# Layers two and three of the last MLP as fp32r products in a two-layer graph network kernel

## The reference

```python
def conv(x, a, eps, W, b):               # GIN block
    ax = a @ x
    h = ax + (1.0 + eps[0]) * ax
    for i in range(3):
        h = relu(h @ W[i].T + b[i])
    return h
merged = concatenate((conv(x, adj, eps1, W1, b1), conv(x2, adj, eps2, W2, b2)), axis=1)
x = layernorm(x + merged @ Wm.T + bm)    # layer 0 of the network
A = adj + eye(4096); deg = A.sum(axis=1)
d = where(deg > 0, rsqrt(deg), 0)
x = layernorm(x + ((d[:, None] * A * d[None, :]) @ x) @ W.T + b)   # layer 1
```

## Time and profile before

| | |
|---|---|
| median of three runs | 594.1 us |
| the profiled execution's own time | 593.58 us |
| its span in the trace | 591.8 us |
| TensorE busy | 584.8 us (99%) |
| VectorE busy | 540.5 us (91%) |
| ScalarE busy | 372.2 us (63%) |
| mean granted TensorE clock | 0.997 |

### The profile page before, as it was taken

How to read it: one execution, slowest core, us unless ns; L and a number is a source line. 1 busy time by engine, 2 the same in 40 slices (tenths; PEclk the granted TensorE clock), 3 DMA queues, 4 the chain that set the end, 5 groups by cost and what they waited for, 6 DMA issues and landing times.

```text
span 591.8 us, 7721 instructions
## 1 busy us (share of the span) xinstructions
PE 584.8 (99%) x2676; PEld 484.3 (82%) x2676; DVE 540.5 (91%) x679; ACT 372.2 (63%) x494; POOL 28.7 (5%) x31
## 2 busy tenths in 40 slices
PE   8999999999999999999999999999999999999996
PEld 7888888888888888888888888867888888888885
DVE  6999999997988998998799999994899999989986
ACT  6554446842544773454667336486897888898893
POOL 1000000001100000110000020000200010010011
PEclk9999999999999999999999999999999999999998
DMA  9978565443554533354443375776699999999911
GB/s 334 370 271 296 202 226 197 142 148 137 214 205 170 190 145 142 142 213 174 181 150 138 138 293 189 286 299 212 245 353 413 364 370 383 400 365 374 387 42 71
DMA packets 27849, 141.56 MB, mean 239 GB/s; under 512 B 2608, under 2 KB 3376, under 8 KB 13616
## 3 DMA queue, kind: packets, MB, share of 16 engines
q1 hardware_dynamic: 27248, 139.54, 63.6%
q10 hardware_dynamic: 576, 1.70, 0.7%
HBM read 139.14 MB, written 2.10 MB: 239 GB/s over the span
## 4 chain that ended last, share of the span: by engine, by line
PE 98%; issue 0%; DVE 0%; POOL 0%; POOLq 0%; DVEq 0%
PE ps L468 81%; PE ps L544 7%; PE pd L486 6%; PE pd L497 2%; PE pd L530 1%; PE pd L592 1%; POOLq L118 0%; POOL rstd L1119 0%; DVE z L1090 0%; PE pd L494 0%; DVE stats L1095 0%; DVE outn L1104 0%; POOL identity L1123 0%; DVE mv L897 0%; DVEq L118 0%
## 5 line engine op out<-in xcount | busy, mean ns | idle before, releaser
L649 ACT ACTIVATE ahi<-raw 128x1024 fp32r<-128x1024 f32 x212 | 221.7, 1057 | 165.4 <-PE ps L468 152.8
L816 DVE TENSOR_TENSOR alo<-raw,ahi 128x1024 fp32r<-128x1024 f32 x212 | 257.2, 1220 | 29.7 <-ACT ahi L649 27.9
L468 PE MATMUL ps<-ahi,x2s 128*128 128x512 f32 x512 | 138.4, 389 | 0.0
L468 PE MATMUL ps<-ahi,x1hi 128*128 128x512 f32 x384 | 121.8, 393 | 0.0
L468 PE MATMUL ps<-alo,x1hi 128*128 128x512 f32 x384 | 120.5, 390 | 0.0
L468 PE MATMUL ps<-ahi,x1lo 128*128 128x512 f32 x384 | 120.4, 389 | 0.0
L468 PEld LDWEIGHTS ps<-ahi,x2s 128*128 128x128 f32 x512 | 96.1, 188 | 20.0
L468 PEld LDWEIGHTS ps<-ahi,x1hi 128*128 128x128 f32 x384 | 71.9, 188 | 15.9 <-issue 1.4
L468 PEld LDWEIGHTS ps<-alo,x1hi 128*128 128x128 f32 x384 | 72.0, 188 | 15.2 <-DVE alo L816 0.3
L468 PEld LDWEIGHTS ps<-ahi,x1lo 128*128 128x128 f32 x384 | 72.1, 188 | 14.9
L468 PE MATMUL ps<-alo,x2s 128*128 128x512 f32 x256 | 80.3, 389 | 0.0
(11 more groups left out here) (98 smaller groups left out, 510.7 us busy)
## 6 DMA issues: line engine op xcount, KB each, us to landing
raw<-a_t SPq DMA_DIRECT2D x108, 1024.0 KB, 4.9
raw<-a_t SPq DMA_DIRECT2D x32, 512.0 KB, 7.4
raw<-early SPq DMA_DIRECT2D x7, 512.0 KB, 7.8
xn<-x SPq DMA_DIRECT2D x3, 1024.0 KB, 8.1
out<-outn ACTq DMA_DIRECT2D x3, 512.0 KB, 6.7
par<-params SPq DMA_DIRECT2D x1, 708.0 KB, 12.8
raw<-head SPq DMA_DIRECT2D x2, 256.0 KB, 3.2
xn<-x SPq DMA_DIRECT2D x1, 512.0 KB, 7.2
```

What stands on the lines that cost most here:

```text
L468: mm = pe.matmul(ps[bank + (CH * (q % 2) if layer else 0)][:, :], block_of(w, n), a[c], start=(n == 0 and k == 0), stop=(n == JB - 1 and k ...
L649: act.activation(ring_hi(layer, q, n), raw_tile(layer, n), ACT.Copy).then_inc(hi_ready, 1)
L816: dve.tensor_tensor(ring_lo(layer, q, n), raw_tile(layer, n), as_f32(ring_hi(layer, q, n)), ALU.subtract).then_inc(lo_ready, 1)
```

## The change

In plan 1, dense layer 0 stays a float32 product. Dense layers 1 and 2 become three fp32r passes each. After relu 0 and relu 1 of each part, ScalarE makes a second relu from PSUM with output in fp32r (hhi). VectorE subtracts it from h into h_rest, which lies on h's own place. Slots four and five of the ring of high parts get memory of their own instead of hhi's, one of them on the place of rowsum_all; rounding of tile 5 therefore waits for the transpose, which moves from VectorE's step 4 to step 1, and the reduction from 5 to 2.

TensorE's dense layers come after tiles 1, 3 and 5 and the merge after tile 6. ScalarE's relus stay after tile 7 for layer 0, and go from 8 and 9 to 9 and 10 for layers 1 and 2. VectorE's remainders of h come at the ends of its steps 4 and 6, the residual after tile 11 instead of 10, and ScalarE's normalising starts at 15 instead of 14.

```diff
@@ -66,26 +66,27 @@
 
 
 
-PE_DENSE = ({3: 0, 5: 1, 8: 2}, {1: 0, 2: 1, 3: 2})
-PE_MERGE = (10, 4)
+PE_DENSE = ({3: 0, 5: 1, 8: 2}, {1: 0, 3: 1, 5: 2})
+PE_MERGE = (10, 6)
+DVE_SPLIT_H = {4: 1, 6: 2}
 PE_PROJECT = 1
 PE_WARM = 8
 
 
 AHEAD_OF_PE = (SPLIT, SPLIT2)
 ACT_EVACUATE = (2, 2)
-ACT_RELU = tuple({k + ahead: l for k, l in plan.items()} for plan, ahead in zip(PE_DENSE, AHEAD_OF_PE))
-DVE_RESIDUAL = tuple(k + ahead for k, ahead in zip(PE_MERGE, AHEAD_OF_PE))
+ACT_RELU = ({k + SPLIT: l for k, l in PE_DENSE[0].items()}, {7: 0, 9: 1, 10: 2})
+DVE_RESIDUAL = (PE_MERGE[0] + SPLIT, PE_MERGE[1] + SPLIT2 - 1)
 STATISTICS = (2, KB)
 TB = 32
 GROUPS = P // TB
 DVE_AGGREGATE = (DVE_RESIDUAL[0] + 1 + KB // STATISTICS[0], DVE_RESIDUAL[1])
 DVE_DEGREES = tuple(k + 1 for k in DVE_RESIDUAL)
-DVE_TURN = (5, 4)
+DVE_TURN = (5, 1)
 DVE_BASE = 10
 DVE_BASE_LAST = 20
 DVE_SHIFT = tuple(k + 2 for k in DVE_AGGREGATE)
-ACT_NORM = (22, 14)
+ACT_NORM = (22, 15)
 ACT_COPY_AY = 3
 DVE_MAKE_Y = (KB + 4, 2 * KB + 4, 3 * KB + 3, 18)
 NORM_BLOCKS = (2, 2)
@@ -140,11 +141,15 @@
         x2hi, x2lo = x2s[:, :, 0, :], x2s[:, :, 1, :]
         xn = sb("xn", [P, QUARTERS, QW])
         raw = sb("raw", [P, RAW, 2, QW])
+        with ExitStack() as until_turned:
+            rowsum_all = until_turned.enter_context(nc.sbuf_tensor("rowsum_all", [P, QW], F32))
+        ahi_extra = [sb(f"ahi_extra{i}", [P, QW], F32R) for i in range(SPLIT2 - SPLIT)]
+        with ExitStack() as whole:
+            h = whole.enter_context(nc.sbuf_tensor("h", [P, M, CW], F32))
+        h_rest = sb("h_rest", [P, M, CW], F32R)
         ahi = sb("ahi", [P, SPLIT, QW], F32R)
         alo = sb("alo", [P, SPLIT, QW], F32R)
-        h = sb("h", [P, M, CW])
         hhi = sb("hhi", [P, M, CW], F32R)
-        rowsum_all = sb("rowsum_all", [P, QW])
         partial = sb("partial", [P, QW // TB])
         own = sb("own", [P, QW // TB])
         degree = sb("degree", [P, KB])
@@ -307,10 +312,7 @@
         def ring_hi(layer, q, n):
 
             i = slot(layer, q, n)
-            if i >= SPLIT:
-                m = 2 * (i - SPLIT)
-                return hhi[:, m:m + 2, :].rearrange("p m w -> p (m w)")
-            return ahi[:, i, :]
+            return ahi[:, i, :] if i < SPLIT else ahi_extra[SPLIT2 - 1 - i][:, :]
 
         def ring_lo(layer, q, n):
 
@@ -478,6 +480,9 @@
                     if plan == 0:
                         wait(pe, hlo_ready, q * (LAYERS * M) + (M * l + m + 1))
                         passes = ((whi, hhi), (whi, hlo), (wlo, hhi))
+                    elif l:
+                        wait(pe, hlo_ready, q * (LAYERS * M) + (M * (l - 1) + m + 1))
+                        passes = ((whi, hhi), (whi, h_rest), (wlo, hhi))
                     else:
                         wait(pe, h_ready, q * (4 * M) + (M * l + m + 1))
                         passes = ((par, h),)
@@ -645,6 +650,8 @@
                         if n // KB == q:
                             act.wait_ge(identity_added, identities(q, n))
 
+                if layer == 1 and q == 0 and n == SPLIT2 - 1:
+                    act.wait_ge(turned_ready, QUARTERS)
                 wait(act, block_used, used_ahead(layer, q, n))
                 act.activation(ring_hi(layer, q, n), raw_tile(layer, n), ACT.Copy).then_inc(hi_ready, 1)
 
@@ -671,6 +678,9 @@
                                    bias=par[:, at:at + 1]).then_inc(h_ready, 1)
                     if plan == 0 and l < LAYERS - 1:
                         round_h(q, l + 1, m)
+                    if plan == 1 and l < LAYERS - 1:
+                        act.activation(hhi[:, m, :], pd[:, m, :], ACT.Relu,
+                                       bias=par[:, at:at + 1]).then_inc(hhi_ready, 1)
 
             def normalise(done, dst, ready, blocks):
 
@@ -830,10 +840,12 @@
                     to = rowsum_all if n == JB - 1 else rowsum
                     dve.tensor_tensor(to[:, :], rowsum[:, :], tile, ALU.add).then_inc(raw_used, 1)
 
-            def split_h(q, l, m):
-
-                wait(dve, hhi_ready, q * (LAYERS * M) + (M * l + m + 1))
-                dve.tensor_tensor(hlo[:, m, :], h[:, m, :], as_f32(hhi[:, m, :]),
+            def split_h(q, l, m, plan):
+
+                if plan == 1:
+                    wait(dve, h_ready, q * (4 * M) + (M * l + m + 1))
+                wait(dve, hhi_ready, q * (LAYERS * M) + (M * (l - plan) + m + 1))
+                dve.tensor_tensor((hlo, h_rest)[plan][:, m, :], h[:, m, :], as_f32(hhi[:, m, :]),
                                   ALU.subtract).then_inc(hlo_ready, 1)
 
             def residual_base(q):
@@ -913,10 +925,10 @@
                 if plan == 0:
                     if n in (ACT_EVACUATE[0] + 1, ACT_EVACUATE[0] + 2):
                         for m in range(CH):
-                            split_h(q, 0, CH * (n - ACT_EVACUATE[0] - 1) + m)
-                    if n in ACT_RELU[0] and ACT_RELU[0][n] < LAYERS - 1:
-                        for m in range(M):
-                            split_h(q, ACT_RELU[0][n] + 1, m)
+                            split_h(q, 0, CH * (n - ACT_EVACUATE[0] - 1) + m, 0)
+                if plan == 0 and n in ACT_RELU[0] and ACT_RELU[0][n] < LAYERS - 1:
+                    for m in range(M):
+                        split_h(q, ACT_RELU[0][n] + 1, m, 0)
                 if n == DVE_TURN[plan]:
                     turn_rowsums(q)
                 if n == DVE_TURN[plan] + 1:
@@ -1050,6 +1062,9 @@
                     elif q == 0:
                         if n + AHEAD < KB:
                             add_identity(q, n + AHEAD)
+                        if n in DVE_SPLIT_H:
+                            for m in range(M):
+                                split_h(LAST, DVE_SPLIT_H[n], m, 1)
                     elif (n + AHEAD2) // KB == q:
                         add_identity(q, n + AHEAD2)
```

## The result

The changed kernel takes 597.52 us (median of 6 runs, 596.82 to 597.98), the kernel before 594.25 us (6 runs, 594.02 to 594.75). The ratio is 1.0054, 95% interval 1.0041 to 1.0067: slower by 2.4 to 4.0 us. The forecast had the sign and ScalarE's part of the loss right, but 595.9 us and the range to 597.4 are too low.

What follows compares the result with a forecast made beforehand. TensorE was taken to bound the kernel, with ScalarE setting the stage's pace: merge end 415.7 against 413.95, 1.75 us lost where 1.5 were to be won. 594.1 + 1.8 = 595.9 us, range 594.0 to 597.4.

Steps and rivals of the forecast that it cites:

- Saving: TensorE's dense layers 1 and 2: three fp32r passes take 2.75 us each, saving 1.45 us; at most 1.5 to be had.
- VectorE's order up to relu 0: From split of tile 1 to identity 7: 7.74 us, reduction now ahead, so ScalarE begins relu 0 at 397.28, not 396.79.
- ScalarE's chain: Relu 0 to the merge: 20 relus and 3 roundings, 14.3 us, set the pace; 1.75 us lost.
- After the merge: VectorE's residual, statistics and split of tile 14, moved later, still reach TensorE in time, with 1 us to spare.
- D: Rival, after the merge: VectorE comes later than the 1 us margin allows, 1 to 2 us more lost, 597.5; chance 0.14.
- B: Rival, at the merge's start: not slower, ScalarE's queue shorter than reckoned; break-even at 410.15, time 593.1 or 592.6; chance 0.09.
- C: Rival, second layer: the delay is taken back later by a load or queue that bounds it, 594.1; chance 0.08.
- E: Rival, dense 1 to the merge: the clock falls in TensorE's new waits, about +8 us, 602; chance 0.04.

Runs made afterwards that it cites:

- e3_no_second_relu: The changed kernel without ScalarE's second relu, so the rounding of h for layers 1 and 2 is left out: 594.62 us against 594.65 for the kernel before.
- e8b_all: The changed kernel with half of h made on VectorE, the row-sum reduction behind identity 7 and the last y a tile later: 592.85 us against 594.78 before.
- e1: The changed kernel's order and memory kept, but dense layers 1 and 2 single float32 products again: 595.65 us against 594.65 for the kernel before.
- e5: The changed kernel with the last y rounded by ScalarE after tile 20 and split by VectorE after tile 21: 596.41 us against 594.78 before.
- e7: The changed order and memory with float32 products, and the last y a tile later: 594.13 us against 594.78 for the kernel before.

## Why the prediction was wrong

**Saving.** Right. 1.5 us was the most to be had, and e3_no_second_relu and e8b_all have it (-1.51, -1.52).

**VectorE's order up to relu 0.** Right. Sum 7.74 was forecast from the split of tile 1 to the end of identity 7; it is 397.46 - 389.79 = 7.67, and ScalarE starts relu 0 at 398.46, 4.54 after dense 0 (forecast 397.28 - 392.71 = 4.57).

**ScalarE's chain.** Right in mechanism and nearly in size: 1.75 us lost was forecast, 1.90 measured. The second relu costs the 0.57 us taken, from start to start. The missing 0.15 us is not late work. Counted from dense 0, tile 7 was forecast at 415.7 - 392.71 = 22.99 and came at 23.01. But the forecast compared its 415.7 with 413.95, the end of tile 6 by its place on the chain, and in TensorE's own row tile 7 starts at 413.82, which is 0.13 earlier; the other 0.02 is the forecast's. That it is so little is partly luck, as two errors nearly cancel: the merge starts at 19.10 (forecast 19.19), and from there to tile 7 it takes 3.91 (3.79 taken).

**After the merge.** This is the step that failed: "Covered, with 1 us to spare". It was worked out for tile 14 and held there (0.8 us were left). The chain of VectorE's later duties was not followed to its end: what comes behind tile 14 was put at nothing. The number that was needed stands in the trace of before. VectorE splits tile 20 there after a wait for ScalarE, then y, and tile 21 right behind y:

```profile
429.61 1.23 DVE L816 TENSOR_TENSOR alo<-raw,ahi 128x1024 fp32r<-128x1024 f32 x1 [0.94 <-ACT ahi L649]
430.75 1.22 DVE L959 TENSOR_TENSOR x1lo<-yt,x1hi 128x1024 fp32r<-128x1024 f32 x1
431.89 1.22 DVE L816 TENSOR_TENSOR alo<-raw,ahi 128x1024 fp32r<-128x1024 f32 x1
```

It has the low part of tile 21 at 433.11. TensorE's tile 21 starts 14 tiles after tile 7, at 413.82 + 14 x 1.361 = 432.87, and needs the low part after four matmuls, at 433.78. The margin was 0.67 us. The change moves the merge behind two more tiles, which costs VectorE 2.72 us of lead at the residual, and it gets one split (1.14 us) done in exchange: 1.58 us less margin. 0.67 - 1.58 = -0.91. In the trace after, split 21 is done at 437.84 and TensorE would need it at 416.93 + 14 x 1.361 + 0.91 = 436.89, 0.95 late. The same sum for tile 20 gives a margin of 1.58 us before and of nothing after: its split is done at 435.57, 0.04 after the 435.53 at which it was needed. TensorE's rows say what each costs: behind tile 20 it is 0.22 us late against its pace from tile 7 on, and behind tile 21 1.12 us, all but 0.02 of the 1.14 in the table. e1 shows that the order alone brings it, e5 and e7 that it is y's place ahead of these splits.

**The rivals.** D was this place in the abstract, "VectorE comes later than the 1 us of margin allows", at 597.5, with a chance of 0.14. It should have been in the forecast. That its number is the measured time is luck: it rested on 2 to 3 us of delay and 1 to 2 lost, without the deadline at tile 21, and 1.14 were lost. B, C and E did not happen. B: the merge starts 19.10 us after dense 0, and it would have had to start at 410.15 - 392.71 = 17.44. C: nothing is taken back; at tile 22, behind the last of the new waits, the kernel is 3.03 us behind the one before, and at the last residual 3.04. E: the granted clock stayed at 1.00, its higher level of 2.4 GHz, in all four stretches of 4 us from 398 to 414; two of them (busy PE, PEld, DVE, ACT, POOL, then clock):

```profile
398.00:402.00 4.00, 3.52 (x14) 2.28 (x13) 1.38 (x2) 4.00 (x8) 0.00 (x0) 1.00 0.64 256
...
406.00:410.00 4.00, 3.81 (x17) 2.66 (x15) 2.52 (x5) 4.00 (x8) 0.00 (x0) 1.00 0.74 262
```

TensorE's idle times there are up to 0.3 us each. Over 434 to 438, with the 0.61 us ahead of tile 21's low part, it was 1.00 as well. What the Trainium skill ("TensorE: Matmul & The Clock Gate", "A second HAM failure mode: psum-queue depth-cycling") tells of another kernel, that frequent short idle times between groups of matmuls made the clock swing, does not show here.

**The median.** Traces from dense 0 give +3.04, the timed medians +3.27. The difference is inside the interval. The spans' difference of 4.3 us would have misled: 1.21 of it is the start.

## What to carry to other kernels

When a step is moved later in one engine's order, work out the margin of every later deadline of the engines that feed it, down to the last duty that stands ahead of a tile, not only the first; the margin that decided here was 0.67 us, seven tiles behind the one that I had cleared. A cheaper product is only cheaper if the engine that prepares its operands has the time: 1.5 us on TensorE was paid with 4.6 us of relus on ScalarE while VectorE stood idle beside it, and moving half of h's relus there, with one reduction put behind what others wait for and y a tile later, turned 3 us of loss into 1.5 of gain. Compare traces from a common mark shortly ahead of the change, not by their spans.

## What the runs showed of the hardware

A relu of 128 x 512 from PSUM costs 0.57 us on ScalarE from start to start whether it writes float32 or fp32r; rounding it from SBUF costs 0.52 (two of them from 398.97 to the next start at 400.01 in e8b_all). VectorE's add and maximum from PSUM costs 0.65 (two from 396.74 to 398.05).

With ScalarE busy without a break, its recorded durations grow (0.67 to 0.79 us for a relu, 1.06 to 1.20 for a rounding of 128 x 1024) while its pace does not change; after an idle time a rounding is back at 1.06. The results come with the recorded ends, so they come later too: VectorE's remainder starts 0.10 us after the recorded end of the second relu both at 399.81 and at 409.80. I had taken durations as constant.

From a common mark, two profiles of one kernel agree within 0.03 us over 190 us (both kernels, two profiles each), while the mark itself lies between 392.71 and 394.28 us in the twelve profiles.
